# Products as scalar-tensor-tensor instructions, and a new order by hand on all five engines

## The reference

```python
# 1. deformable sampling: 1024 grid queries per image, 8 sampling points each
q_feat  = bilinear_sample(feature_map, ref)            # at the grid's points
off     = (gelu(layer_norm(q_feat @ W_o1 + b_o1)) @ W_o2 + b_o2) * 4
sampled = bilinear_sample(feature_map, ref + off * scale)
#   = v00*(1-wx)*(1-wy) + v01*wx*(1-wy) + v10*(1-wx)*wy + v11*wx*wy
keys, values = sampled @ W_k.T, sampled @ W_v.T        # softmax over the 8 points
# 2. h = concat(sampled tokens, txt): 1152 tokens; h += causal_attention(layernorm(h))
# 3. h += ffn(layernorm(h)): top 2 of 16 experts, 64 -> 128 -> 64, relu,
#    weighted sum, then layer norm with gamma and beta
```

## Time and profile before

| | |
|---|---|
| runs, us | 4530.77, 4535.62, 4522.31; median 4530.77 |
| the profiled execution, us | 4536.96, its span on the core 4534.9 |
| granted TensorE clock, mean | 0.885 |
| PE busy | 3669.2 us, 81% of the span |
| DVE busy | 3077.4 us, 68% |
| ACT busy | 2199.1 us, 48% |
| POOL busy | 3203.0 us, 71%; 3072 indirect DMAs |
| DVE's products, lines `weigh` and `weigh_rest` | 512, 619.2 us, 1218 ns each |
| first gather; steady passes; end | 121.8 us; about 534 to 4129 us; 4534.9 us |

### The profile page before, as it was taken

The page is one execution under the profiler, slowest core; times in us unless marked ns, Lnnn a source line. Parts: engine busy times, 40 slices in busy tenths (PEclk is TensorE's granted clock), DMA queues, the critical chain, the costliest instruction groups (busy, mean ns, idle before and its releaser), DMA issues.

```text
span 4534.9 us, 82922 instructions
## 1 busy us (share of the span) xinstructions
PE 3669.2 (81%) x26592; PEld 3201.3 (71%) x26592; DVE 3077.4 (68%) x9228; ACT 2199.1 (48%) x5378; POOL 3203.0 (71%) x3089
## 2 busy tenths in 40 slices
PE   4577988888888888888888888888888888877863
PEld 2466877777777777777777777777777777766752
DVE  0485858677695858778595867759586876957331
ACT  2254555455555545554555545455554555544411
POOL 0777677777777777777777777777777777777142
PEclk9888998899989989998999999899899999888755
DMA  8669686776958677686858677685867768542322
GB/s 249 214 188 249 182 262 190 237 215 198 281 142 274 175 238 216 196 256 169 266 165 255 201 226 221 183 268 152 266 183 242 214 200 273 146 143 82 87 71 58
DMA packets 938629, 911.26 MB, mean 201 GB/s; under 512 B 121306, under 2 KB 822362, under 8 KB 938072
## 3 DMA queue, kind: packets, MB, share of 16 engines
q1 hardware_dynamic: 805768, 598.22, 44.1%
q0 software_dynamic: 132432, 307.74, 23.1%
HBM read 583.69 MB, written 323.53 MB: 200 GB/s over the span
## 4 chain that ended last, share of the span: by engine, by line
POOL 30%; PE 27%; issue 12%; DMA 10%; DVE 10%; SPq 6%; ACT 5%; POOLq 0%; DVEq 0%; ACTq 0%
POOL gath L760 14%; POOL xs_d L776 11%; POOL ya L792 5%; DMA fm<-in_x 5%; PE ps L869 3%; PE ps L883 3%; PE ps L814 3%; PE ps L966 3%; PE ps L1034 3%; PE ps L1026 2%; DMA xg<-xs_d 2%; PE ps L944 2%; SPq L705 2%; SPq L674 2%; DMA gath<-table,idx 1%
## 5 line engine op out<-in xcount | busy, mean ns | idle before, releaser
L760 POOL DMA_INDIRECT gath<-table,idx x2048 | 2131.9, 1041 | 790.1 <-issue 649.2
L792 POOL DMA_INDIRECT ya<-ys_d,row x512 | 527.1, 1030 | 355.7 <-DMA ys_d<-yx 189.6
L1234 DVE TENSOR_TENSOR prod<-gath,corner_w 128x1024 f32<-128x1024 f32 x512 | 619.2, 1218 | 214.7 <-DMA gath<-table,idx 194.6
L869 PE MATMUL ps<-const,prod 128*128 128x128 f32 x4096 | 601.9, 295 | 111.1 <-DVE prod L1234 108.9
L883 PE MATMUL ps<-w_kv,samp_t 128*128 128x128 f32 x4096 | 627.5, 302 | 53.3 <-ACT kv_sb L1050 42.3
L776 POOL DMA_INDIRECT xs_d<-xm,row x512 | 534.4, 1044 | 168.2 <-issue 155.2
L883 PEld LDWEIGHTS ps<-w_kv,samp_t 128*128 128x128 f32 x4096 | 571.4, 215 | 81.2 <-issue 62.2
L869 PEld LDWEIGHTS ps<-const,prod 128*128 128x128 f32 x4096 | 520.6, 155 | 145.4 <-DVE prod L1234 120.2
L944 PE MATMUL ps<-k_t,q_t 128*128 128x512 f32 (+3 forms) x960 | 415.8, 525 | 103.8 <-ACT v_sb L1050 67.7
L1234 DVE TENSOR_TENSOR yx<-ps,wx 128x256 f32<-128x256 f32 x320 | 134.1, 419 | 538.6 <-PE ps L1034 538.2
L1050 ACT ACTIVATE rows<-ps 128x512 f32<-128x512 f32 x512 | 304.3, 594 | 356.0 <-PE ps L814 355.1
(11 more groups left out here) (168 smaller groups left out, 6134.9 us busy)
## 6 DMA issues: line engine op xcount, KB each, us to landing
table<-rows SPq DMA_DIRECT2D x224, 1024.0 KB
fm<-in_x SPq DMA_DIRECT2D x256, 512.0 KB
wx<-w_d SPq DMA_DIRECT2D x768, 128.0 KB
gath<-table,idx POOLq DMA_INDIRECT x2048
wx<-w_d SPq DMA_DIRECT2D x64, 512.0 KB
table<-rows SPq DMA_DIRECT2D x32, 960.0 KB
xg<-xs_d SPq DMA_DIRECT2D x192, 130.0 KB
ys_d<-yx SPq DMA_DIRECT2D x192, 128.0 KB
```

The source lines that it names most:

```text
L760: pool.indirect_dma_start(out=gath[:, n % NG, p, :], out_offset=None, in_=tables[par], in_offset=bass.IndirectOffsetOnAxis(ap=idx[:, par, ...
L792: pool.indirect_dma_start(out=ya[:, k, t, :], out_offset=None, in_=ys_d[par], in_offset=bass.IndirectOffsetOnAxis(ap=row[:, par, n:n + 1], ...
L869: last = pe.matmul(bank(0, p * P, p * P + P), prod[h][:, (p * 2 + dx) * P:(p * 2 + dx + 1) * P], ident, is_transpose=True, start=(dx == 0) ...
L1234: return dve.tensor_tensor(o, a, b, op)
```

## The change

The two products are written with `stt`, the gathered corners times 1.0 times the weights, from and into the same buffers with the same semaphores. All strings of `TURNS` and `LAST` are replaced. They have the same letters in other places; POOL's and SP's are given here in full, with before and after in the diff (those of the other engines are left out).

```diff
@@ TURNS @@
     "gpsimd":
-        "pppppppffffffffffffffffpppffffffffffffffffccccccccccccccccccccccccccccccccpppppp",
+        "pppppppffffffffffffffffpfpfffffpffcfffccffcccfccccfcccfccccccccpcccccccccccppppp",
     "sync":
-        "ggxxgxxgxgxxxggxgxgxxhxgxxxgggggggggggxxgehgxgxxxexxxxxx",
+        "ggxxxggxxxgxggxxxggxxxxxgghxggxgxxxggggggxeggxxxhxexxxxx",
@@ LAST @@
     "gpsimd":
-        "pppppppffffffffffffffffpppffffffffffffffffccccccccccccccccccccccccccccccccppffffffffffffffffffffffff"
-        "ffffffffccccccccccccccccccccccccccccccccffffffffffffffffffffffffffffffff",
+        "pppppppffffffffffffffffpfffpfffffpccccfffccfcccffffcccccccccccccccccccccccppffffffffffffffffffffffff"
+        "fffffffccfccccccccccccccccccccccccccccccffffffffffffffffffffffffffffffff",
...
@@ weigh @@
-                tt(prod[0][:].rearrange("p (n c) -> p n c", c=C), g,
-                   cw.unsqueeze(2).to_broadcast([P, 16, C]), ALU.mult).then_inc(wcorn[0].sem, 1)
+                stt(prod[0][:].rearrange("p (n c) -> p n c", c=C), g, 1.0,
+                    cw.unsqueeze(2).to_broadcast([P, 16, C]), ALU.mult, ALU.mult).then_inc(wcorn[0].sem, 1)
@@ weigh_rest @@
-                tt(prod[1][:].rearrange("p (n c) -> p n c", c=C), g,
-                   cw.unsqueeze(2).to_broadcast([P, 16, C]), ALU.mult).then_inc(wcorn[1].sem, 1)
+                stt(prod[1][:].rearrange("p (n c) -> p n c", c=C), g, 1.0,
+                    cw.unsqueeze(2).to_broadcast([P, 16, C]), ALU.mult, ALU.mult).then_inc(wcorn[1].sem, 1)
```

More of the change, by code:

```diff
@@ L256 @@
-        "vwxaxxaavaevvvxavxeeeeeeeggeeeaeeewxaeevevgeeeaeeeveexgxaagxxageexxexgxxgavxavwaaxvavvvxvvawvvvvvvva"
-        "vxxawvxvvavwaxaaaaaaaawaaaaaavvvvvvxvvvvvvvvaaaaaaaaxaaaavvaaa",
+        "wawaaaaawaaaxaawaaaavwxwvvvaaxwawvvaavxvavvavvaxawawvaavvxvvavavvwxwavvvvvvvxvaaawwvavxaavvavwwvaaav"
+        "avvavavvawvaavvaaaaaaaaaaaaaavaawvvvevvveevevaeaaaeaavevvavavwwveavevaaavaeeevraawvavvwvrearrrvaraar"
+        "aaaeaearrvaaeeerreaaarevxvrvrvvvwwgeggggeveggeggggggegggggegggaggwvxexeaeaxvxavaavaxvvxxvexeaeagexva"
@@ L258 @@
+        "veaegeeaxegvewxexaveaaexegevegvgwgeaeeeexgavvvegvxgeaeeeagxwaxaxavavvxaaaexvxvxaaevxvvwvvxvaxxvvvxax"
+        "vvxawwavaavxaaaavaaaaaaaaavwvvvvevvvxvvvvaavaaavavaaxaaaavaava",
     "gpsimd":
-        "pppppppffffffffffffffffpppffffffffffffffffccccccccccccccccccccccccccccccccpppppp",
+        "pppppppffffffffffffffffpfpfffffpffcfffccffcccfccccfcccfccccccccpcccccccccccppppp",
     "sync":
-        "ggxxgxxgxgxxxggxgxgxxhxgxxxgggggggggggxxgehgxgxxxexxxxxx",
+        "ggxxxggxxxgxggxxxggxxxxxgghxggxgggxggggggxeggxxxhxexxxxx",
@@ L264 @@
     "tensor":
[L265 to L268, removed]
+        "xxtxtxktktaxatxaaxakasxssqxaxstktxkqtxqxasxkxsxtxaqtxksxaxskxqxsqxsktxqaxktxasxaqqtsqtsaktssqaaqaqak"
@@ L269 @@
+        "qakqaataakakaktkttkktrtxkxxktaxataaaksaxssqstqaxsaxksqasqxsxaskqtsxqaqxsattksqxkaxqassxqqakxxsqatxax"
+        "qqkatqakxaatxtxkxtkaxakaxaxxxxxxxaaxaaxaaxssxsqxsxaqxxaqxsxqxasxsxxsxaxqxxsqxqsxaxxsqaasqaqsqssaqaqa"
+        "qaqaaaaaaarxxxxxxxxxxxxxxxxxxxxxxxxxxxxxxxxxxxxxxxxxxxxxxxxxxxxx",
     "scalar":
-        "xxttkxtakatxaaaaataxavkxstqsxkxtsvqxqkxstxkxtsxqvxksxqtxkqtqkxtvxsqktqtsqvkqqskqqqtaavkaakaatvktktkt"
-        "vaktktxkvaxaaataakxaaeeeavstsqxqskqtssqxqvkqkxtsqstkexqtkeeqxsvqqqxstkvqqktqvxxtkxtkxaavktaakaaxvxax"
@@ L272 @@
-        "xxaaxaaaaaaxaxsqsxxsqxqxsxxsxqxsxqxqqxxsqqsqqqsqqqaaaaaaaxxxeeexxxexeexxxxxxxxxxxxxxxxxxxxxxxxxxeeee"
+        "xxttkxtakatxaaaaaxvatkasxsqtsxkxtvqxtqkxsxtsxqkxkvxsqxqktxtkxtqvxsqqtktskvqqsqqkqqktavaakakaatvkttkk"
+        "tvaktvtkxxtaaaakaaxeaaeeastvqsskqxsqktqxvstqkqsxsqttkxeeqevsqqxkqqxsktvqqktqxvtkxxtkxaavtkaaakaxxvxa"
+        "xxaaaxaaaaxaaxsqxssxqsxxqxxqxxssqxxqqxxsqqqsqsqqqqaaaaaaaxxeeexxxxeexxexxxxxxxxxxxxxxxxxxxxxxxxxeeee"
         "ee",
     "vector":
-        "wawaaxawwaaaaaaaaaaawvvxwwvvaaxvvwaavvvvvvxavavxaavwaawaavxvvvavawxwavvvaxaavvvwwvvavvvvaxvvvvaawaav"
@@ L281 @@
-        "xxeexxexxxxxxxxxxxxxxxxxxxxxeeeeeeeeeeeeeeeeeeeeeeeeeeeeeeeeeeeeeeeeeeeeeeeeeeeeeeeeee",
+        "waawaxaaawaaaaaaaawawvxvvwwvaaxvvavaavwwvvvvxaavavvxvwaaavvvaxvavawxwvaavvvavwvxvawvaxvaavvvvawvwava"
+        "aavvaaaavvavwvaaaaaaaaaavaaaaaavwvvvvveevevveevaavveawaeaeawvevavaeeaeaavavrveaveavawvvaraerraveeaea"
+        "vraavervaaaaaerrrwvraaawvvxerwerrvreexeexvevwveaavxeaaavavxvaxavvaxavaxxxvevvaeaxwaeeaevxeeeaeexevxa"
+        "eavwxeaeeevexeexeeeeeeeaxavavxeaeavexxxvavaxvxxwaxvavvxavwvvvvvavaxvvwvxaavwaxaaaaaxaawaavaaavvavvvv"
```

25 lines of the change are left out of this document (10 added, 15 removed).

## The result

| | before | after |
|---|---|---|
| median of 4 runs, us | 4532.9 (4522.3 to 4535.6) | 4662.7 (4657.1 to 4668.9) |
| profiled execution, us (span) | 4536.96 (4534.9) | 4668.86 (4666.9) |
| granted TensorE clock, mean | 0.885 | 0.858 |

The ratio of the times is 1.0275, with a 95% interval from 1.0251 to 1.0299. The change costs 130 us. 4538 was predicted, with a range of 4465 to 4625.

The account below looks back on a forecast made before the run. POOL was taken to bound the kernel, its 192 indirect DMAs filling a steady pass of 259 us. The terms 0 + 0 + 7 + 0 + 0 = +7 gave 4544 us against the profiled execution, 4538 against the median, range 4465 to 4625.

Parts of the forecast that it names:

- (1): DVE's two products in the new opcode: still 1218 ns each, 0 us, bounds nothing and +0.5%.
- (2): Hold of POOL's DMAs by DVE's products: the new form holds like the old, 0; lower end -182 us.
- rival C: The new form of the products doesn't hold POOL: up to -182 us, a third given back, 4410 us; chance 0.07.
- (3) first point, the 17th fetch: POOL's 17th fetch, slot 96 to 80, waits 0.5 us for `ya_rd`: +7 us in 14 passes.
- Second point, the first scatter: POOL's first scatter, slot 112 to 104, 10.8 us earlier; 3.9 us are left before it would wait: 0.
- Fourth point, the last scatter: POOL's last scatter, slot 143 to 151, delays SP's `xg` loads; PE may stand 0 to 2 us: 0.
- (3) third point, the last fetch: POOL's last fetch, slot 111 to 124, 17.5 us later; DVE stands 7.3 us at `combine(1)`, covered: 0.
- The cover: DVE's later waits for gathered data, 8.9 us a pass, shrink by DVE's lateness; without this +7.3 per pass.
- the 28.5 us of waits at the sixth p: POOL's gathers wait for weighed tiles at the sixth of the first seven p: 28.5 us over the run.
- (4) the other strings: New orders of PE, ACT, DVE and SP, reaching POOL through `wcorn`: 0, bounds -28 to +102 us.
- (5) holds: Holds of POOL shift with the order, no reason for a sign: 0, 28 us either way.
- rival A: DVE's and PE's lateness reaches POOL's gathers: 4589 us, whole 4640; sign, POOL's extra idle over 5 us a pass; chance 0.23.

Follow-up runs that it names:

- e1: Kernel before with the two products as scalar-tensor-tensor, in the old order: 4535.3 us, ratio 1.0006.
- e7: Kernel before with both products replaced by a TENSOR_REDUCE of the same length that reads one SBUF tensor: 4475.6 us, ratio 0.9884.
- e10c: Kernel before with 13 scatters put ahead of the last 13 fetches in POOL's steady string, last fetch at slot 124: 4664.2 us, ratio 1.0278.
- e4: Kernel before with only POOL's steady string taken from the kernel after: 4622.5 us, ratio 1.0201.
- e9: Kernel before with one tile of gathers put ahead of the last 11 scatters in POOL's string: 6736.6 us in the first batch, ratio 1.0007.

## Why the prediction was wrong, step by step

**(1) and (2), the opcode: right.** Products 1217 ns against 1218, the hold of 0.82 us, and `e1` at 1.0006. The rival C (no hold at all) would not have given the 4410 us that I priced but 4476, as `e7` shows: of the 13 us a pass that I took for the holds, 11.7 were there, but I gave back a third where 8.4 of 11.7 come back.

**(3) first point, the 17th fetch: too dear by half a microsecond a pass.** It never waited for `ya_rd` in a steady pass of after, so the +7 of the sum was 0. **Second point, the first scatter: right** in after; in `e10c` the same working, 17.5 against 14.7, gives the 3 us that were measured. **Fourth point, the last scatter: nearly right**, 0 against 0.2%.

**(3) third point, the last fetch: the step that failed.** It was wrong twice.
- The size. I had DVE stand for 17.5 + 1.5 - 11.7 = 7.3 us. It stood for 11.4 to 13.4 in the steady passes of `e10c` and for 12 to 15 in those of after. The 1.5 us from the end of the fetch to the start of `ya` came from a stretch with few other DMAs around it (at 4073, where the DMA engines are busy for 0.15 of the time); in the passes of `e10c` it is 3.4 to 4.6, and in the one shown the DMA engines are busy all that time. That their load makes the difference is likely and not shown. With this and with the 3.1 us that the scatters stood ahead of the fetch, the same sum gives 17.5 + 3.1 + 4.0 - 11.7 = 12.9 for `e10c`. For after it gives 17.5 + 4.4 - 11.7 = 10.2, and where its other 2 to 5 us come from stays open.
- The cover. "The cover is DVE's later waits for gathered data" was looked up on DVE alone. Those waits did shrink, by 7.9 us a pass. But PE and ACT stood with DVE, at the attention of the same pass, and the whole compute side was late together, with PE at the lower clock behind the stand.

The deeper error stands in the first part: "PE has 37 us of slack." POOL's time does fill the pass. But the earlier trace rows and the 28.5 us of waits at the sixth p said that a second chain was as long: a bound engine that stands at the same place in 10 of 12 passes is being met there by another. That chain runs through all of PE, ACT, DVE and SP's loads, waits included, so no busy share shows it. It had 3 us to spare, and DVE's stand of 12 to 15 us exceeds that. In `e4`, which has the late fetch without the new compute order, the stand is 8.5 to 11.9 us, 9.8 in the mean; less 3 this leaves 6.8, and the pass is 6.6 us longer. That the two agree so well is partly luck, as the slower clock isn't in this sum.

**(4) the other strings: "between them I take 0": wrong, and with it the bound.** The compute strings alone cost 143 us with POOL's and SP's old ones. I had bounded them above by what DVE's lateness from (3) could carry, +102. A cost of their own, from PE's, ACT's and DVE's places against one another and against SP's loads, wasn't in the bounds at all. I had written of them that most steps move by under ten places; with 3 us of slack in a pass ten places may be much. (Both upper bounds, here and in C, multiply by 14 passes; 13 have all 192 instructions, so that +102 should have been +95.)

**(5) holds: right.** Busy time of POOL 199.7 us a pass before and 199.4 after.

**The rival A was the right mechanism**, with 0.23. That DVE's lateness adds up until POOL stands at the sixth p of the next pass is what the timeline shows; its sign, over 5 us of POOL's idle time a pass, came true with 12.8. The point from which I said it decides, some 9 us, should have been 3. Its upper price, 4640, lies 23 us under the result; the compute strings' cost under (4) wasn't in it. That the price is so near is partly luck: the lateness was undersized and taken 14 times.

## What to carry to other kernels

Before a change of order is called covered, look for the second chain. If the bound engine waits for the others at one place in nearly every pass, those others have little slack, whatever their busy shares say (here 3 us a pass), and a longer wait put into one of them can arrive there. And when a DMA's result is asked for later in a hand-written order, look at moving its reader with it: here the last fetch went 13 slots later and its reader stayed. No run moved the reader, so what that would have saved isn't shown.

## What the runs showed of the hardware

- The hold of an indirect DMA by a DVE instruction depends on the second SBUF tensor and not on opcode or length: TENSOR_TENSOR and SCALAR_TENSOR_TENSOR of 1024 elements hold (end + 0.82 to 0.83 us), a TENSOR_REDUCE of 1024 elements doesn't (946 ns under it), nor does a TENSOR_TENSOR with one of its tensors in PSUM (951 ns in the median). Taking away the products' holds is worth 53 us here, though it takes 188 us from POOL's busy time (3203.0 to 3014.7).
- When PE stands at `combine(1)` the granted clock falls from 1.00 to 0.50 and stays there while PE works again: eight matmuls of line 869 take 1.91 us and, once it is back, 1.04.
- The same kernel can run half as long again on a chip for a while. In two batches before took 6733 us (25 runs) and 6899 us (18 runs), with all its runs within 1.2% of each other; one of the two chips ran it in 4540 us later. In the trace of `e9` in the first of these ACT stands for 20.90 us with a releaser that the profile doesn't see, while the DMA engines are nearly idle (the first line is a piece of 10 us of that time, with the columns of the earlier trace rows; the second is ACT's instruction behind it):

```profile
3000.00:3010.00 10.00, 0.58 (x1) 0.29 (x1) 0.00 (x0) 0.00 (x0) 7.56 (x9) 0.50 0.14 26
```

```profile
3016.45 0.28 ACT L1050 ACTIVATE qft<-ps 128x128 f32<-128x128 f32 x1 [20.90 <-remote]
```

The cause is open.
